# Gathering twelve small tables jointly at the head of a recommendation tower on one Trainium2 core

## The reference, cut to what matters

```python
e = stack([tbl_f[ids[:, f]] for f in range(32)], axis=1)      # [512, 32, 64] f32, 32 tables of 1000 to 125000 rows
# CIN, two layers:  hidden = x = e
z = einsum('bhd,bfd->bhfd', hidden, x)                        # layer 1: 32 x 32, layer 2: 64 x 32 channels
y = relu(einsum('bcd,oc->bod', z.reshape(B, -1, D), w) + b)   # w0 [128, 1024], w1 [128, 2048]
# layer 1: the first 64 outputs are the next hidden, the last 64 are summed over d; layer 2: all 128 are summed
h = concat([sums, dense_ctx], axis=1)                         # [512, 192 + 16]
y = relu(relu(h @ W_top1 + b_top1) @ W_top2 + b_top2) @ W_top3
```

## Time and profile before

| | us |
|---|---|
| median of 3 runs | 1043.92 |
| lowest and highest | 1043.32, 1044.97 |
| the profiled execution | 1043.1 |
| its span | 1041.3 |
| granted TensorE clock, mean over the span | 0.989 of full |

### The profile page before, as it was taken

The page is one execution under the profiler, slowest core; times in us unless marked ns, Lnnn a source line. Parts: engine busy times, 40 slices in busy tenths (PEclk is TensorE's granted clock), DMA queues, the critical chain, the costliest instruction groups (busy, mean ns, idle before and its releaser), DMA issues.

```text
span 1041.3 us, 11554 instructions
## 1 busy us (share of the span) xinstructions
PE 1001.6 (96%) x3561; PEld 669.6 (64%) x3561; DVE 932.4 (90%) x806; ACT 789.7 (76%) x951; POOL 916.3 (88%) x310
## 2 busy tenths in 40 slices
PE   2399999999999999999999999999999999999999
PEld 1146566666667666676667676767676767676773
DVE  3089999999999999999999999999999999999981
ACT  5057676678888888888888888878888888788772
POOL 6619888899999999999999999999999999999980
PEclk9599999999999999999999999999999999999999
DMA  6498887777877877878787778778766676767620
GB/s 175 87 240 196 193 195 182 195 186 185 197 185 194 189 190 183 191 190 193 183 200 183 188 187 193 189 179 196 193 167 173 174 184 172 172 174 194 158 70 0
DMA packets 140833, 184.20 MB, mean 177 GB/s; under 512 B 55698, under 2 KB 56338, under 8 KB 140643
## 3 DMA queue, kind: packets, MB, share of 16 engines
q1 hardware_dynamic: 136178, 179.19, 70.2%
q0 software_dynamic: 4096, 4.20, 2.3%
q10 hardware_dynamic: 496, 0.06, 0.0%
HBM read 174.92 MB, written 8.39 MB: 176 GB/s over the span
## 4 chain that ended last, share of the span: by engine, by line
PE 94%; issue 3%; POOL 1%; DMA 1%; SPq 1%; DVE 0%; ACT 0%; DVEq 0%
PE py L797 35%; PE py L818 16%; PE py L806 16%; PE py L807 16%; PE py L827 3%; PE py L833 3%; PE py L826 2%; PE py L838 1%; POOL emb L404 1%; SPq L304 0%; DMA xs<-x_dram 0%; PE pzB L897 0%; PE pzS L897 0%; DMA emb<-in_tbl,idx 0%; DVE zf L683 0%
## 5 line engine op out<-in xcount | busy, mean ns | idle before, releaser
L415 POOL TENSOR_TENSOR zl<-zf,zh 128x2048 fp32r<-128x2048 f32 x178 | 783.8, 4418 | 67.0 <-ACT zh L483 65.6
L683 DVE TENSOR_TENSOR zf<-xs,hid 128x2048 f32<-128x2048 f32 (+1 forms) x256 | 537.6, 2109 | 32.9 <-ACT hid L513 24.7
L483 ACT ACTIVATE zh<-zf 128x1536 fp32r<-128x1536 f32 (+1 forms) x184 | 338.3, 1838 | 90.3 <-DVE zf L683 87.3
L797 PE MATMUL py<-zf,wf 128*128 128x512 f32 x860 | 390.8, 592 | 1.6 <-DVE zf L683 1.5
L806 PE MATMUL py<-zh,wh 128*128 128x512 f32 x736 | 287.0, 390 | 0.0
L807 PE MATMUL py<-zh,wl 128*128 128x512 f32 x736 | 286.4, 389 | 0.0
L797 PEld LDWEIGHTS py<-zf,wf 128*128 128x128 f32 x860 | 162.2, 189 | 156.1 <-issue 141.7
L818 PE MATMUL py<-zl,wh 128*128 128x512 f32 x736 | 225.5, 428 | 0.0
L818 PEld LDWEIGHTS py<-zl,wh 128*128 128x128 f32 x736 | 138.4, 188 | 57.3 <-issue 32.5
L404 POOL DMA_INDIRECT emb<-in_tbl,idx x128 | 132.4, 1034 | 29.1 <-issue 26.1
L806 PEld LDWEIGHTS py<-zh,wh 128*128 128x128 f32 x736 | 138.1, 188 | 29.6 <-issue 0.2
(11 more groups left out here) (104 smaller groups left out, 651.2 us busy)
## 6 DMA issues: line engine op xcount, KB each, us to landing
xs<-x_dram SPq DMA_DIRECT2D x512, 256.0 KB
xs<-x_dram SPq DMA_DIRECT2D x252, 64.0 KB
xt_pair<-x_dram SPq DMA_DIRECT2D x128, 64.0 KB
x_pair<-x_dram SPq DMA_DIRECT2D x128, 64.0 KB
x_dram<-emb SPq DMA_DIRECT2D x66, 64.0 KB
x_dram<-emb SPq DMA_DIRECT2D x22, 96.0 KB
emb<-in_tbl,idx POOLq DMA_INDIRECT x128
x_dram<-emb SPq DMA_DIRECT2D x4, 384.0 KB
```

The costliest lines, as they stand in the source:

```text
L415: pool.tensor_tensor(zl[:, q, first:T], zf[:, s, first:T], zh[:, q, first:T].bitcast(F32), ALU.subtract).then_inc(lo["P"], 1)
L483: act.activation(zh[:, q, first:T], zf[:, s, first:T], ACT.Copy).then_inc(hi, 1)
L683: dve.tensor_tensor(zf[:, slot(u), first:T], left[:, first:T], view(right, at, [[0, T - first], [1, N]]), ALU.mult).then_inc(mult, 1)
L797: mm = pe.matmul(y, wf[:, w, h], zf[:, s, h], start=first and h == first_tile, stop=ends and h == T - 1)
```

## The change

Tables 20 to 31 (`JOINT` = 20, `NJ` = 12) are copied by twelve DMAs from DRAM to DRAM into one tensor `table_joint`. An index tensor `idx_joint` of 96 partitions (12 tables by 8 samples) and 3 columns (groups 0, 1, 2) is made on VectorE: the ids, loaded in that layout, plus the first row of each table. Three joint gathers then fetch, for groups 0, 1 and 2, the rows of all twelve tables, 96 rows each.

The order on GpSimd becomes: fields 0 to 19 of chunk 0, one gather each (batches of 12, 5 and 3), then the three joint gathers, then fields 20 to 31 of all of chunk 0, each waiting for the gather before it to land, then the periods.

The first three batches are stored for groups 0 to 2 only (24 partitions of `emb`), and the joint rows after them. The other groups of chunk 0 are stored later, all 32 fields at once, in two stages (`store_stage`): groups 3 to 6, and groups 7 to 15. The loads of group 3 (x0, xd and the pairs) wait for the first stage, and in SyncE's order they stand behind `load_xd(2)` and `load_xe(1)`. On ScalarE `copy_x0(3)` and `copy_xt(2)` move to the end of period 1. From group 4 on the loop is as before, except for one wait for the second stage.

B of group 0 becomes whole. TensorE takes B before D in period 0 too, turns the dense inputs first, and warms up with three matmuls instead of four. The weights of the top layers are loaded at group 50.

The emb buffer is read by `c` instead of `c % 2` for the first batches, which is the same for chunk 0; `pad` grows from 16 to 208 columns.

```diff
-    if name in "PD" or unit in (("A", 0), ("C", 0)):
+    if name in "PD" or g == 0:
         return "F"
...
-FIRST_BATCHES = [(0, 0, 12), (0, 12, 12), (0, 24, 5), (0, 29, 3)]
+JOINT = 20
+NJ = F - JOINT
+JOINT_GROUPS = 3
+FIRST_BATCHES = [(0, 0, 12), (0, 12, 5), (0, 17, 3), (0, JOINT, NJ)]
+REST = len(FIRST_BATCHES) - 1
+STAGES = [JOINT_GROUPS, 7, GC]
...
+            sp.dma_start(dense[:], dense_ctx.rearrange("(c p) n -> p c n", p=P)).then_inc(dense_in, 16)
+            for k in range(JOINT_GROUPS):
+                first = ids[NS * k:NS * k + 1, JOINT:JOINT + 1]
+                sp.dma_start(ids_joint[0:NS * NJ, k:k + 1], bass.AP(tensor=first.tensor, offset=first.offset, ap=[[1, NJ], [F, NS], [1, 1]]),
+                             allow_slow_non_contiguous=True).then_inc(ids_joint_in, 16)
...
+            for j in range(NJ):
+                sp.dma_start(table_joint[offsets[j]:offsets[j + 1], :], tables[JOINT + j]).then_inc(tables_joined, 16)
...
             def store_batch(n):
                 c, f, m = BATCHES[n]
                 sp.wait_ge(gathered[n % BATCH_SEMS], gathered_count(n))
-                if n == 3:
-                    sp.wait_ge(x32_cleared, 2)
-                    load_x32(sp, 31, x32_last)
+                if n < REST:
+                    if n == 2:
+                        sp.wait_ge(x32_cleared, 2)
+                        load_x32(sp, f + m - 1, x32_last)
+                    for i in range(REPEATS):
+                        dst = x_dram[c, i * F + f:i * F + f + 1, :]
+                        sp.dma_start(bass.AP(tensor=dst.tensor, offset=dst.offset, ap=[[D, NS * JOINT_GROUPS], [P * D, m], [1, D]]),
+                                     emb[0:NS * JOINT_GROUPS, c, f:f + m, :]).then_inc(x_stored[c], 16)
+                    return
...
+            def store_stage(k):
+                if k == 0:
+                    for n in range(REST + 1):
+                        sp.wait_ge(gathered[n], gathered_count(n))
+                lo, hi = NS * STAGES[k], NS * STAGES[k + 1]
+                for i in range(REPEATS):
+                    dst = x_dram[0, i * F:i * F + 1, D * lo:D * lo + 1]
+                    sp.dma_start(bass.AP(tensor=dst.tensor, offset=dst.offset, ap=[[D, hi - lo], [P * D, F], [1, D]]),
+                                 emb[lo:hi, 0, :, :]).then_inc(stage_stored[k], 16)
+
+            def store_joint(k):
+                sp.wait_ge(joint_gathered[k], 16)
+                if k == 0:
+                    sp.dma_start(x32[JOINT:F, :], emb_joint[0:NS * NJ, 0]).then_inc(x32_last, 16)
+                for i in range(REPEATS):
+                    sp.dma_start(x_dram[0, i * F + JOINT:i * F + F, N * k:N * k + N], emb_joint[0:NS * NJ, k]).then_inc(joint_stored[k], 16)
...
-            for n in range(len(FIRST_BATCHES)):
+            for n in range(REST):
                 store_batch(n)
+            for k in range(JOINT_GROUPS):
+                store_joint(k)
 
             sp.wait_ge(w_turned, 6)
             sp.wait_ge(x_stored[0], 16 * STORES[0])
+            sp.wait_ge(joint_stored[0], 16 * REPEATS)
             load_xd(0)
+            sp.wait_ge(joint_stored[1], 16 * REPEATS)
             load_x0(1)
             load_xd(1)
+            sp.wait_ge(joint_stored[2], 16 * REPEATS)
             load_xt_pair(1)
             load_x0_pair(1)
             load_xe(0)
             load_x0(2)
-            for g in range(G):
+            load_xd(2)
+            load_xe(1)
+
+            store_stage(0)
+            sp.wait_ge(stage_stored[0], 16 * REPEATS)
+            load_x0(3)
+            load_xt_pair(2)
+            load_xd(3)
+            load_x0_pair(2)
+            store_batch(batch_of(0))
+            load_xe(2)
+            store_stage(1)
+            load_x0(4)
+            for g in range(2, G):
+                if g == 4:
+                    sp.wait_ge(stage_stored[1], 16 * REPEATS)
+                if g == 50:
+                    load_top()
...
+                if n == REST and i > 0:
+                    pool.wait_ge(gathered[n], 16 * i)
...
+            def gather_joint(k):
+                if k == 0:
+                    pool.wait_ge(idx_joint_ready, 1)
+                    pool.wait_ge(tables_joined, 16 * NJ)
+                pool.indirect_dma_start(
+                    out=emb_joint[0:NS * NJ, k, :], out_offset=None, in_=table_joint[:],
+                    in_offset=bass.IndirectOffsetOnAxis(ap=idx_joint[0:NS * NJ, k:k + 1], axis=0),
+                ).then_inc(joint_gathered[k], 16)
+
             for n, (_, _, m) in enumerate(FIRST_BATCHES):
+                if n == REST:
+                    for k in range(JOINT_GROUPS):
+                        gather_joint(k)
                 for i in range(m):
                     gather(n, i)
...
-                    if g + 2 < G:
+                    if g != 1 and g + 2 < G:
                         copy_x0(g + 2)
-                if g % 2 and g + 2 < G:
+                if g > 1 and g % 2 and g + 2 < G:
                     copy_xt(g // 2 + 2)
...
+                if g == 1:
+                    copy_x0(3)
+                    copy_xt(2)
...
-            warm_up(4, py1[:])
-            pe.wait_ge(x32_in, 16 * (2 * NS + 5))
-            pe.wait_ge(x32_last, 16 * 3)
+            warm_up(3, py1[:])
+            pe.wait_ge(x32_in, 16 * (NS + 5))
+            pe.wait_ge(x32_last, 16 * 4)
```

More of the change, by code:

```diff
@@ L62 @@
 BATCH_SEMS = 4
-STORES = [sum(min(m, REPEATS) for b, _, m in BATCHES if b == c) for c in range(NC)]
+STORES = [sum(min(m, REPEATS) for n, (b, _, m) in enumerate(BATCHES) if b == c and n != REST) for c in range(NC)]
 def gathered_count(n):
@@ L224, in dlrm_tower @@
         x_dram = nc.dram_tensor("x_dram", [NC, REPEATS * F, P * D], F32, kind="Internal")
-        ids_in, consts_in, top_in = sem("ids_in"), sem("consts_in"), sem("top_in")
+        offsets = [sum(t.shape[0] for t in tables[JOINT:JOINT + j]) for j in range(NJ + 1)]
+        table_joint = nc.dram_tensor("table_joint", [offsets[NJ], D], F32, kind="Internal")
+        ids_in, consts_in, top_in, dense_in = sem("ids_in"), sem("consts_in"), sem("top_in"), sem("dense_in")
+        ids_joint_in, tables_joined, rows_set, idx_joint_ready = sem("ids_joint_in"), sem("tables_joined"), sem("rows_set"), sem("idx_joint_ready")
+        joint_gathered = [sem("joint_gathered%d" % k) for k in range(JOINT_GROUPS)]
+        joint_stored = [sem("joint_stored%d" % k) for k in range(JOINT_GROUPS)]
+        stage_stored = [sem("stage_stored%d" % k) for k in range(len(STAGES) - 1)]
         eye_in, w0_in, w1_in = sem("eye_in"), sem("w0_in"), sem("w1_in")
@@ L374, in _ @@
                         load_xt_pair(g // 2 + 2)
-                if g == 0:
-                    load_xd(g + 2)
                 if g + 3 < G:
                     load_x0(g + 3)
-                if 0 < g < G - 2:
+                if g < G - 2:
                     load_xd(g + 2)
-                if g >= 1 and batch_of(g - 1) is not None:
+                if batch_of(g - 1) is not None:
                     store_batch(batch_of(g - 1))
@@ L539, in finish_2 @@
                 act.activation(py2[:, g % 2], py2[:, g % 2], ACT.Relu, bias=bias1[:]).then_inc(dir2_ready, 1)
[L541 to L545, removed]
-            act.wait_ge(gathered[2], gathered_count(2))
-            for f in range(24, 29):
-                load_x32(act, f, x32_in)
-            act.wait_ge(gathered[3], gathered_count(3))
-            for f in range(29, 31):
-                load_x32(act, f, x32_last)
+            _, f, m = FIRST_BATCHES[0]
+            act.wait_ge(gathered[0], gathered_count(0))
+            for b in range(NS):
+                act.dma_start(x32[f:f + m, D * b:D * b + D], emb[b:b + 1, 0, f:f + m, :]).then_inc(x32_in, 16)
+            _, f, m = FIRST_BATCHES[1]
+            act.wait_ge(gathered[1], gathered_count(1))
+            for i in range(m):
+                load_x32(act, f + i, x32_in)
+            _, f, m = FIRST_BATCHES[2]
+            act.wait_ge(gathered[2], gathered_count(2))
+            for i in range(m - 1):
+                load_x32(act, f + i, x32_last)
             act.wait_ge(x_spread, 1)
@@ L760, in _ @@
             pe.wait_ge(eye_in, 16)
+            pe.wait_ge(dense_in, 16)
+            for c in range(NC):
+                tr = pe.transpose(px0[0:16, P * c:P * c + P], dense[:, c, :], ident[:])
+            tr.then_inc(dense_turned, 1)
             pe.wait_ge(w0_doubled, 8)
@@ L769, in _ @@
             pe.transpose(pzS[:, 0:P], sym16, ident[:]).then_inc(w_turned, 1)
-            pe.wait_ge(top_in, 16 * 8)
-            for c in range(NC):
-                tr = pe.transpose(px0[0:16, P * c:P * c + P], dense[:, c, :], ident[:])
-            tr.then_inc(dense_turned, 1)
             def bank(u):
@@ L875, in _ @@
                 main(("C", g))
-                for name in "DB" if g == 0 else "BD":
-                    main((name, g))
+                main(("B", g))
+                main(("D", g))
                 late(("C", g))
```

(1 more changed line is left out.)

49 lines of the change are left out of this document (36 added, 13 removed).

## The result

The changed kernel takes 1058.22 us (median of 4 runs, 1057.32 to 1059.77), the kernel before 1043.62 (1043.22 to 1044.97) beside it. The ratio is 1.0137 [1.0124, 1.0149]. The forecast was 1040 with a range of 1030 to 1049, so both the time and the side were wrong. The profiled execution took 1058.29 us, of which the span is 1056.5, against 1043.1 and 1041.3.

A forecast was written before the change was run, and what follows sets the result against it. TensorE was taken as the bound, busy 1001.6 of 1041.3 us. From 1043.1, minus 12.75 (head), plus 0.7 (B of group 0 whole), plus 8.5 (stall) gave 1039.5, 1040 as a median; range 1030 to 1049.

The forecast's parts named there:

- Part 1: Head: with 20 gathers and three joint ones, the spreading matmuls start at 35.9 instead of 48.65, 12.75 us earlier.
- Rival (b): Head: table copies from DRAM to DRAM end late and delay the joint gathers; 1046 to 1052 us, chance 0.20.
- The loads at 35.6: Head: the first loads start when the joint stores end their issue, at 35.6, 14.9 us earlier than 50.46.
- Part 3: After the joint gathers: the late single gathers and the SyncE work behind them stall TensorE by 8.5 us.
- G: Moment the last of chunk 0's twelve serial single gathers is seen: 72 us, lower bound 63, upper bound 78.
- (c): Single gathers take 4.8 us under load, G is 78, stall 14.5, the clock falls: 1045 to 1048; chance 0.20.
- Behind G: SyncE's queue after G, in order: x0(4) lands at about G + 23, C of group 2 ready at G + 25.5.
- The stall formula: TensorE before C of group 2: ready at G + 25.5, wanted at 89.0, so G - 63.5, or 8.5 us.
- Rival (a): Single gathers keep near 2.46 us under load, G is 63 to 65, stall 0 to 1.5: 1032; chance 0.22.
- the order of what is late: Group 2 and GpSimd's lows behind G: stalls of 8.5 us for C, 5.3 for lows, 3.6 for A, not added.

The follow-up runs named there:

- f1: The kernel before with the twelve DRAM-to-DRAM copies added and read by nothing: 1043.76 us, ratio 1.0.
- f2: e4 without the twelve copies, the joint gathers reading rows of table 20 instead: 1040.63 us, ratio 0.9967.
- e4: The changed kernel with single gathers not waiting for each other and x0(4) loaded ahead of the second stage store: 1041.05 us, ratio 0.9969 in its first comparison.
- e5: e4 with copy_x0(1) on ScalarE behind the finishing steps of group 0: 1057.67 us, ratio 1.014.
- e6: e4 with the first stage store ahead of load_xd(2), its landing awaited behind load_xe(1): 1053.1 us, ratio 1.0082.
- g2: e4 with the edits of e5 and e6 together: 1036.17 us, ratio 0.9922.
- f3: e4 unchanged, run a third time: 1040.57 us, ratio 0.9968.
- e1: The changed kernel with the twelve single gathers no longer waiting for each other: 1043.32 us, ratio 0.999.
- g1: e6 run again in a later comparison: 1038.43 us, ratio 0.9944.
- r_e4: e4 unchanged, run a second time: 1056.25 us, ratio 1.0116.
- e7: e4 with GpSimd waiting for the four DMAs of x0(1) before the rest of chunk 0: 1047.27 us, ratio 1.0041.
- e2b: The changed kernel with two single gathers in flight on alternating semaphores: 1043.61 us, ratio 0.9999.
- f4: The changed kernel with at most two single gathers in flight and x0(4) loaded early: 1041.5 us, ratio 0.9974.
- e3: The changed kernel with x0(4) loaded ahead of the second stage store: 1056.14 us, ratio 1.0119.

## Why the prediction was wrong, by its steps

**Part 1, the head: right.** 35.85 was measured for 35.9, and tail 0 is 12.8 us early for 12.75. The copies ended by 22 us: 3.65 MB from 9.1 to 21.9 us, 284 GB/s where I took 290. Of the 322 GB/s from 10 to 20 us their queue had 305, and the gathers beside them the rest:
```profile
q1 hardware_dynamic: 324, 3.05, 91.5%
```
These are packets, MB and share of the time of 16 engines, from 10 to 20 us. Rival (b) falls by the joint gather that did not wait, and by f1 and f2. The Trainium skill's rule (page "DMA: Bandwidth & Descriptors", section "Why a DMA increments its semaphore by 16 and not by 1"), taken with 1250 and 1000 rows as the slowest dimension, gave 10 engines. The trace does not agree with that reading: ten engines can fill at most about 0.63 of the time of 16, where this queue has 0.92, and each table went as 16 packets, of 20000 B for 1250 rows and 16000 B for 1000. The same passage of the skill goes on that software can split a contiguous access of one dimension into an outer dimension that is a multiple of 16, and the packets look as if each whole table had been taken as one such run. The measurement decides.

**The loads at 35.6: too early by 2.7.** The joint stores took 4.72 us to issue, where I had some 2. With ScalarE's copy_x0(1) standing ahead of the finishing steps and waiting for its load, TensorE waited 4.47 us, and over 50 to 58 the clock was 0.55 and 0.59. I had counted nothing for a fall of the clock here. Together that makes the 5.7 us between tails 0 and 1; how they divide is not shown. In the changed kernel the later stall swallows them, since C of group 2 starts with x0(4) whatever the lead is; in e4 they stay, and e5's and e6's edits together win 1.8 of them (tail 1 at -8.8 in g2 against -7.0 in f3; these two ran in different comparisons, both with a sound head).

**Part 3, G: the step that failed.** I took 4.0 us for a gather under load, from the one row that showed one, and 4.8 as the upper end. The runs show 6.3 to 7.0. G is 83.4 instead of 72: **+11.4 us**, beyond the upper bound of 78. The earlier trace rows gave one sample, and an upper limit of it: SyncE was still issuing a load until 82.34 and then waited only 0.2 us for the gather. It was also a quick one. The trace of the kernel before held a slower one that I did not read, the gather of 86.67. Its 32 packets, by the DMA view of 89.9 to 92.4 and of 92.4 to 92.9 (the view of 86.7 to 89.9 has none):
```profile
86.67 0.96 POOL L404 DMA_INDIRECT emb<-in_tbl,idx  x1
q0 software_dynamic: 25, 0.03, 17.7%
q0 software_dynamic: 7, 0.00, 1.7%
```
The last of them moved over 5.7 us behind the start, at 0.85 of DMA time, while the quick one had 0.95. So the share of DMA time does not by itself tell the latency, and what does is open.

The upper bound was also added up wrongly. Two gathers at 2.46 and ten at 4.8 from 33.3 on give 86.2, not 78. With that, the prediction's own formula gives a stall of 22.7 us and 1053.8 us, so (c) and the top of the range, 1049, were too low by the prediction's own terms, and the measured G lies inside the bound so corrected.

**Behind G.** x0(4) was to land at G + 23; it is seen at G + 28.1, and C of group 2 begins at G + 30.6 (113.95) where I had G + 25.5: **+5.1 us**. The term that was off is the second stage store: 7.35 us of issue, taken at 1.2 as the first one's (0.92 measured), and x0(4) behind it took 4.17 instead of 1.7. Its issue ended at G + 26.2 where I had G + 18.1, 8.1 late; 3.0 of these came back, because it landed 1.9 us behind its issue and not 4.9. The store has 72 partitions by 32 tables, 2304 pieces of 256 B, in each of its two DMAs; the first has 1024. But the number of pieces alone does not set the time: the same two DMAs took 6.91 us in e1, 5.96 in e4, 3.11 in g1 and 3.84 in g2.

**The clock.** The stall formula has C of group 2 as the end: 113.95 - 101.05 is 12.9 us late, and tail 4 is 15.2 late. The remaining **2.3 us** are the half clock of 112 to 116 and shortly after: eleven steps from one matmul to the next, from 113.95 to 118.77, take 0.44 us each instead of 0.23. So 1039.5 + 11.4 + 5.1 + 2.3 = 1058.3, the measured 1058.29. Rival (c) was this mechanism, with its G (78) still too small, and had 0.20. Rival (a) falls by the gathers' steps.

**What was right beside.** The place (a wait behind G, between tails 2 and 4), the order of what is late, and the unchanged steady period. By e1 the serial wait is worth the whole loss: without it the change is at 0.999 of the kernel before, and with x0(4) moved as well at 0.997.

**Open.** What makes the slow head. It came on two of four chips, in every profile taken there of a kernel with the free gathers, weakly with the changed kernel on one, and the time of the kernel before never showed it. The freed gathers do not start it, by the rows of r_e4 and e7, and no run asked what does. Whether their traffic delays the first loads (L) was not told apart either, since e7 ran with a slow head: tail 1 is at -5.8, -6.9 and -7.0 with the free gathers (e1, e4, f3), at -7.4 and -7.2 with two in flight (e2b, f4), and at -7.1 and -8.2 with the serial ones (the changed kernel, e3). If L acts, it is worth no more than some 2 us at tail 1.

## What to carry to other kernels

A chain of waiting DMAs must be priced by latency under the load that will run beside it; one row that shows when somebody saw a completion is one sample, and the other gathers of the same trace (here that of 86.67) must be looked at before it is taken as the price. Before making a transfer wait for the one before it, count the chain: here five links, four of them 6.3 to 7.0 us long, took 18.6 us more than five quiet ones of 2.65, which is more than the head had won (12.8). With two in flight the time was that of the kernel before (ratio 0.9999). And put nothing that the near future needs behind a long wait on an in-order queue: the DMA engines stood at 0.07 for ten us for want of one instruction.

## What was unexpected of the hardware

- A single gather that waits for the one before takes 2.6 to 2.7 us with quiet queues (0.05 to 0.06 of DMA time) and 6.3 to 7.0 beside the first loads (0.72 to 1.06), for 32 KB. The order within the loads does not follow the share: 6.69 us at 0.72, 6.33 at 0.79, and at most 4.0 at 0.95 in the kernel before.
- Copies from DRAM to DRAM of contiguous tables ran at 305 GB/s (322 with the gathers beside them, at 0.98 of DMA time), above the 252 of the loads from x_dram.
- Issuing the same two stores of 2304 pieces of 256 B took SyncE between 3.11 us (g1) and 7.35 us (the changed kernel); two of 1024 pieces took 0.92. The six joint ones, of 96 rows each, took 4.72, and 9.06 in r_e4, but 4.72 in e7 too.
- The same kernel, e4, took 1041.05, 1056.25 and 1040.57 us on three chips while the kernel before stayed at 1043.3 to 1044.8 beside it.
